# Keys by head parity and 64x64 products for the inverse, in a one-core language-model tower

## The reference

```
xr, xw, xk, xv, xa, xg = x + (x shifted by one token - x) * x_r, x_w, ...
r, k, v = xr @ Wr, xk @ Wk, xv @ Wv
w = -softplus(-(w0 + tanh(xw @ w1) @ w2)) - 0.5;  a = sigmoid(a0 + xa @ a1 @ a2);  g = sigmoid(xg @ g1) @ g2
kk = k * k_k, divided by its norm over each head;  k = k * (1 + (a - 1) * k_a)
for each token:  S = S * exp(-exp(w)) + (S @ -kk) (kk * a)^T + v k^T;   y = S @ r
out = (groupnorm(y) + sum(r * k * r_k) * v) * g @ Wo
```

## Time and profile before

| | |
|---|---|
| median of 3 runs | 646.49 us (645.17 to 652.29) |
| profiled execution | 646.06 us, its span 644.3 us |
| TensorE products, weight loads | 12883, 12884 |
| TensorE, VectorE, ScalarE, GpSimd busy | 491.5, 314.6, 236.7, 131.0 us |
| attention | 25.6 to 455.8 us |
| granted TensorE clock, mean | 0.858 |

### The profile page before, as it was taken

The page is one execution under the profiler, slowest core; times in us unless marked ns, Lnnn a source line. Parts: engine busy times, 40 slices in busy tenths (PEclk is TensorE's granted clock), DMA queues, the critical chain, the costliest instruction groups (busy, mean ns, idle before and its releaser), DMA issues.

```text
span 644.3 us, 28157 instructions
## 1 busy us (share of the span) xinstructions
PE 491.5 (76%) x12883; PEld 369.2 (57%) x12884; DVE 314.6 (49%) x686; ACT 236.7 (37%) x411; POOL 131.0 (20%) x117
## 2 busy tenths in 40 slices
PE   0196888798798798798798877786565899999910
PEld 0175676576686686576676666664432456676600
DVE  2356694674674585585565374242625312222213
ACT  2265644544444554453343440033320033333300
POOL 6421070240240140150040040100005400000054
PEclk9998989989888988979979877777785579999965
DMA  7700000000000000000000000000592211121135
GB/s 206 268 2 2 5 3 5 4 5 4 4 5 5 4 4 4 5 3 4 4 5 5 4 4 4 4 4 2 219 419 81 89 40 61 65 65 65 41 103 174
DMA packets 20680, 32.17 MB, mean 50 GB/s; under 512 B 3936, under 2 KB 16218, under 8 KB 20442
## 3 DMA queue, kind: packets, MB, share of 16 engines
q1 hardware_dynamic: 18234, 24.16, 10.6%
q0 software_dynamic: 2336, 6.30, 3.2%
HBM read 20.23 MB, written 10.22 MB: 47 GB/s over the span
## 4 chain that ended last, share of the span: by engine, by line
PE 70%; issue 13%; DVE 6%; ACT 5%; POOL 2%; DMA 1%; SPq 1%; POOLq 0%; DVEq 0%; ACTq 0%
PE ps L1152 7%; PE ps L1169 6%; PE ps L804 5%; PE ps L811 5%; PE ps L816 3%; PE ps L1132 2%; PE ps L825 2%; POOL arena L320 2%; PE ps L879 2%; PE ps L1160 2%; PE ps L872 1%; PE ps L868 1%; PE ps L1068 1%; PE ps L916 1%; PE ps L862 1%
## 5 line engine op out<-in xcount | busy, mean ns | idle before, releaser
L301 POOL TENSOR_TENSOR arena<-arena 128x512 f32<-128x512 f32 x8 | 11.0, 1380 | 244.3 <-ACT arena L394 244.3
L492 DVE SCALAR_TENSOR_TENSOR arena<-arena 128x256 f32<-128x256 f32 x96 | 49.7, 569 | 11.8 <-PE ps L855 8.0
L804 PE MATMUL ps<-arena 128*64 128x128 f32 x512 | 41.0, 327 | 7.7 <-ACT arena L386 4.1
L1152 PE MATMUL ps<-arena 128*128 x92 | 46.3, 628 | 0.1
L804 PEld LDWEIGHTS ps<-arena 128*64 128x64 f32 x512 | 37.3, 169 | 13.3 <-issue 8.9
L1169 PE MATMUL ps<-arena 128*128 x184 | 43.6, 380 | 0.8 <-ACT arena L453 0.8
L759 DVE TENSOR_TENSOR arena<-ps,arena 128x512 f32<-128x512 f32 x23 | 15.9, 692 | 48.0 <-PE ps L1152 48.0
L811 PE MATMUL ps<-arena 128*128 128x256 f32 x128 | 35.4, 423 | 5.1 <-ACT arena L423 5.0
L320 POOL DMA_INDIRECT arena<-sorted_o,arena x16 | 15.7, 980 | 113.4 <-DMA sorted_o<-arena 108.8
L1169 PEld LDWEIGHTS ps<-arena 128*128 128x128 f32 x184 | 33.2, 190 | 5.0 <-issue 1.5
L811 PEld LDWEIGHTS ps<-arena 128*128 128x128 f32 x128 | 25.2, 207 | 10.6 <-ACT arena L423 6.0
(11 more groups left out here) (249 smaller groups left out, 1161.1 us busy)
## 6 DMA issues: line engine op xcount, KB each, us to landing
arena<-W SPq DMA_DIRECT2D x16, 512.0 KB, 10.4
sorted_x<-arena SPq DMA_DIRECT2D x1, 2944.0 KB, 15.6
arena<-sorted_x SPq DMA_DIRECT2D x23, 128.0 KB, 2.0
sorted_o<-arena SPq DMA_DIRECT2D x23, 128.0 KB, 1.7
arena<-b SPq DMA_DIRECT2D x1, 2048.0 KB, 20.2
out<-arena SPq DMA_DIRECT2D x16, 128.0 KB
arena<-W SPq DMA_DIRECT2D x4, 256.0 KB
arena<-consts SPq DMA_DIRECT2D x4, 64.0 KB
```

What stands on the lines that cost most here:

```text
L492: last = V.scalar_tensor_tensor(out=mix[j % 3][:, p, :], in0=xx[:, p].rearrange("p b t -> p (b t)"), scalar=mixed_by[MIXES[j]][:, p:p + 1] ...
L804: last = mul(to, w[:, kt, half(h)], of_parity(src[:, kt, :], e), start=kt == 0, stop=kt == 1)
L1152: last = mm(ps[:, 2 + b, :], x_sT[b][:, p, :], W1_sb[:, bass.ds(e * (2 * HID) + p * HID, HID)], start=p == 0, stop=p == 1)
```

## The change

The change does the following.

- **Layout.** Keys, receptance, decay and the rest now stand as [2 heads x 64 features, chunk, batch, token]: partition half e is the head's parity. `headed` takes 128x128 stationary operands with all 256 columns, the a2 product too; P.cum takes four products with a block-diagonal `tri`; P.rt four products with two columns of `r_k_of`; `to_tokens` is four 128x128 transposes.
- **Inverse.** The products of Q.X and Q.T take two batches at a time: the stationary operand is 64x64, block-diagonal over two batches. For that GpSimd makes `n_w`, N spread over twice the columns (P.masks), and `y_t` is made twice as wide by the masks of VectorE, whose constants `low` and `parity` are widened.
- **P.M, Q.W, Q.S.** Products that read one head's rows run together, one half (or two batches) after the other, and TensorE waits on its own semaphores `m_half`, `w_half`, `s_half` between them.
- **Moved between engines.** ScalarE takes F.xn's two operations, k * k_k, the factor 1 + (a - 1) * k_a, and the floor under the norm (as Relu); GpSimd takes the centring of v (P.vc) and two operations of O.yn; VectorE gives these up.
- **Order.** `ORDER` is new, its numbers go from 3 to -1, and the waits follow it.

```diff
-ORDER = """Q.X0:0 P.vga:1 F.stats:3 Q.T0:0 P.lg:1 Q.A0:-1 P.wup:1 P.vc:0 Q.X1:0 Q.S0:-1 F.xx:2 Q.W1:-1 P.norm:1 Q.T1:0 P.key:1
-P.cum:1 Q.A1:-1 P.rt:0 F.rstd:3 Q.X2:0 Q.S1:-1 O.sq:-1 P.decay:1 P.g:1 O.red:-1 P.k:2 Q.T2:0 P.kP:1 P.ar:1 O.zT:-2
-P.bP:1 P.r:2 Q.X3:0 P.v:2 P.tokk:1 O.yn:-1 O.out:-2 P.M:1 F.xn:3 P.masks:1 P.tokb:1 P.q:1 P.lv:2 Q.T3:0 P.lwa:2
-O.add:-2 Q.W0:0 F.xT:3 P.kk:2""".split()
+ORDER = """P.q:0 Q.X0:0 F.rstd:2 P.r:1 F.xn:2 Q.T0:0 Q.A1:-1 P.norm:1 Q.X1:0 Q.S1:-1 O.sq:-1 O.red:-1 P.v:1 Q.T1:0 P.tokb:0
+P.lv:1 Q.X2:0 O.yn:-1 P.lwa:1 F.xT:2 Q.T2:0 P.vga:1 P.wup:1 Q.W0:0 F.xx:2 P.lg:1 P.key:1 Q.X3:0 O.zT:-1 P.cum:1 Q.T3:0
+P.decay:1 P.rt:1 P.ar:1 P.kP:1 P.bP:1 F.stats:3 Q.A0:0 P.g:1 Q.S0:0 P.k:2 P.M:1 P.masks:1 O.out:-1 Q.W1:0 P.vc:1
+O.add:-1 P.tokk:1""".split()
...
             def headed(w, src, bank):
 
-                for h in range(H):
+                for h2 in range(2):
                     for kt in range(2):
-                        for e in range(2):
-                            to = ps[half(e), bank, :].rearrange("p (h b c t) -> p h b c t", b=2, h=H, c=CH)[:, h]
-                            last = mul(to, w[:, kt, half(h)], of_parity(src[:, kt, :], e), start=kt == 0, stop=kt == 1)
+                        last = mul(pair(ps[:, bank, :], h2), w[:, kt, h2 * 128:(h2 + 1) * 128], src[:, kt, :], start=kt == 0, stop=kt == 1)
...
             def to_tokens(src, bank):
 
                 for c in range(CH):
-                    for h in range(H):
-                        for b in range(B):
-                            g, e, u = h * 2 + b // 2, half(b % 2), c * H + h
-                            last = mul(ps[quarter(b), bank, u * HS:(u + 1) * HS], src[e, g, c, :], ident[e, e], start=True, stop=True)
+                    for h2 in range(2):
+                        last = nc.tensor.transpose(ps[:, bank, c * C + h2 * 128:c * C + (h2 + 1) * 128], chunk(src, h2, c), ident)
...
                 elif step == "P.cum":
...
-                    for c in range(CH):
-                        for h in range(H):
-                            for b in range(B):
-                                q = quarter(b)
-                                to = ps[half(b % 2), 2 + b // 2, h * SL + c * L:(h + 1) * SL]
-                                last = mul(to, sig_w[q, c, half(h)], cst["tri"][q, 0:SL - c * L], start=c == 0 and h == 0, stop=c == 1)
+
+                    for h2 in range(2):
+                        mul(pair(ps[:, 2, :], h2), sig_w[:, 0, h2 * 128:(h2 + 1) * 128], cst["tri"], start=True, stop=False)
+                        last = mul(pair(ps[:, 2, :], h2)[:, 128:256], sig_w[:, 1, h2 * 128:(h2 + 1) * 128], cst["tri"][:, 0:128], start=False, stop=True)
...
                 elif step == "P.M":
...
+                    for hp in range(2):
+                        for part, (src, bank) in enumerate(((bP, 2), (kP, 3))):
+                            if hp:
+                                pe.wait_ge(s["m_half"], 2 * i + part + 1)
+                            for c in range(CH):
+                                for h in (hp, hp + 2):
+                                    for b in range(B):
+                                        u = c * H + h
+                                        last = mul(ps[quarter(b), bank, u * 2 * L:(u + 1) * 2 * L], chunk(src, h // 2, c)[half(hp), quarter(b)],
+                                                   ar[par][half(hp), h // 2, c, b, :], start=True, stop=True)
...
                 elif step == "Q.X0":
                     pe.wait_ge(s["u_ok"], 4 * i + 1)
-                    after(pe, "w_ok", 2 * i - 1)
+                    pe.wait_ge(s["nw_ok"], n)
+                    after(pe, "w_ok", 2 * i)
                     for u in range(UN):
-                        for b in range(B):
-                            q = quarter(b)
-                            last = mul(ps[q, 4, u * L:(u + 1) * L], n_b[par][q, u, 0:L], u_m[q, u, :], start=True, stop=True)
+                        for e in range(2):
+                            last = mul(ps[half(e), 4, u * L:(u + 1) * L], n_w[par][half(e), u].rearrange("p e t -> p (e t)"), u_m[half(e), u, :], start=True, stop=True)
...
+                    for h in (0, 2):
+                        for b in range(B):
+                            last = mul(ps[quarter(b), 4, half(h)], ar[par][half(0), h // 2, 0, b, 0:L], state[half(0), b, h // 2, :], start=False, stop=True)
+                    last.then_inc(s["w_half"], 1)
...
+                    pe.wait_ge(s["w_half"], 4 * i + 1)
+                    for h in (1, 3):
...
+                elif step == "P.masks":
+                    pool.wait_ge(s["nb_ok"], n)
+
+                    P.tensor_tensor(n_w[par], n_b[par][:, :, 0:L].unsqueeze(2).broadcast_to([128, UN, 2, L]), cst["parity"].rearrange("p (e t) -> p e t", e=2).unsqueeze(1).broadcast_to([128, UN, 2, L]), ALU.mult).then_inc(s["nw_ok"], 1)
+                elif step == "O.yn":
+                    pool.wait_ge(s["yn_ok"], n)
+                    P.tensor_tensor(yn, yn, gw[par], ALU.mult).then_inc(s["yg_ok"], 1)
+                    pool.wait_ge(s["yg_ok"], n)
+                    P.tensor_tensor(z, yn, qg[par], ALU.add).then_inc(s["z_ok"], 1)
...
+                elif step == "F.xn":
+                    act.wait_ge(s["res_ok"], n)
+                    act.wait_ge(s["lessm_ok"], n)
+                    for c in range(CH):
+                        last = A.activation(xn[:, c, :], xn[:, c, :], ACT.Identity, scale=rstd[:, c:c + 1], bias=less_mean[:, c:c + 1])
```

More of the change, by code:

```diff
@@ L131, in build @@
         tu = [carve(2, UN, L) for _ in range(2)]
-        y_t = carve(UN, L)
+        y_t = carve(UN, 2, L)
+        n_w = [carve(UN, 2, L) for _ in range(2)]
         w_s, sa = carve(C), carve(C)
@@ L935, in emit @@
                     for u in range(UN):
[L936 to L938 removed]
+                        for e in range(2):
+                            last = mul(ps[half(e), 6, u * L:(u + 1) * L], y_t[half(e), u].rearrange("p e t -> p (e t)"), t_m[half(e), u, :], start=True, stop=True)
                     last.then_inc(s["t_ps"], 1)
@@ L993, in emit @@
-                    for h in range(H):
-                        for b in range(B):
-                            g, e = h * 2 + b // 2, half(b % 2)
-                            last = mul(ps[quarter(b), 4, half(h)], ar[par][e, g, 0, 0:L], state[e, b // 2, half(h)], start=False, stop=True)
+                    for part, bank, at in ((0, 4, 0), (L, 5, 0 * C)):
+                        for h in range(H):
+                            for b in range(B):
+                                q, u = quarter(b), 0 * H + h
+                                mul(ps[q, bank, at + h * HS:at + (h + 1) * HS], m_k[par][q, u, part:part + L], vc[par][q, 0, half(h)],
+                                    start=h == 0 and (part == 0 or 0 == 0), stop=False)
@@ L997, in emit @@
+                    last.then_inc(s["w_half"], 1)
+                    pe.wait_ge(s["w_half"], 4 * i + 1)
+                    for h in (1, 3):
+                        for b in range(B):
+                            last = mul(ps[quarter(b), 4, half(h)], ar[par][half(1), h // 2, 0, b, 0:L], state[half(1), b, h // 2, :], start=False, stop=True)
                     last.then_inc(s["w_ps"], 1)
-                    for h in range(H):
+                    pe.wait_ge(s["w_half"], 4 * i + 2)
+                    for h in (1, 3):
@@ L1039, in emit @@
-                    pe.wait_ge(s["s_ok0"], n)
-                    for h in range(H):
-                        for b in range(B):
-                            g, e = h * 2 + b // 2, half(b % 2)
-                            last = mul(ps[quarter(b), 4, half(h)], ar[par][e, g, 1, 0:L], state[e, b // 2, half(h)], start=False, stop=True)
+                    for part, bank, at in ((0, 4, 0), (L, 5, 1 * C)):
+                        for h in range(H):
+                            for b in range(B):
+                                q, u = quarter(b), 1 * H + h
+                                mul(ps[q, bank, at + h * HS:at + (h + 1) * HS], m_k[par][q, u, part:part + L], vc[par][q, 1, half(h)],
+                                    start=h == 0 and (part == 0 or 1 == 0), stop=False)
@@ L1044, in emit @@
+                    last.then_inc(s["w_half"], 1)
+                    pe.wait_ge(s["w_half"], 4 * i + 3)
+                    for h in (1, 3):
+                        for b in range(B):
+                            last = mul(ps[quarter(b), 4, half(h)], ar[par][half(1), h // 2, 1, b, 0:L], state[half(1), b, h // 2, :], start=False, stop=True)
                     last.then_inc(s["w_ps"], 1)
-                    for h in range(H):
+                    pe.wait_ge(s["w_half"], 4 * i + 4)
+                    for h in (1, 3):
@@ L1213 @@
     col = np.arange(L)
+    pos = np.arange(B * SL)
+    heads, none = a[P + "r_k"], np.zeros((HS, 1), np.float32)
     f = np.float32
```

374 lines of the change are left out of this document (188 added, 186 removed).

## The result

The changed kernel takes **595.17 us** (median of 4 runs, 588.21 to 597.56) where the kernel before, on the same chip, takes 645.83: a ratio of 0.913, 95% interval 0.9004 to 0.9255. The ratio is taken over the faster executions of each kernel (590.7 and 647.0 us in the mean) and so is lower than 595.17 / 645.83 = 0.922. Forecast were 621 us; the sign was right and the gain was twice the forecast one.

What follows compares the result with a forecast made beforehand. TensorE's work and instruction delivery together were taken as the bound. A turn of 44.4 + 0.5 + 1.0 = 45.9 us against 49.96 brought attention from 430.2 to 405.5, hence 621 us; own range 606 to 636, 8 in 10 592 to 656.

Steps and rivals of the forecast that it cites:

- the end of the pauses: TensorE's idle time on instruction delivery in a steady turn: 0.5 us left of 6.7.
- the other waits: TensorE's waits for other engines, such as P.norm's table load and GpSimd's steps before O.zT: 1.0 us a turn added.
- the cover I was least sure of: GpSimd's widened N (1.5 us) before Q.X0: hidden by TensorE's work, but the one exposed first if that cover went.
- the clock term: TensorE in the steady turn: without pauses part of the lost clock returns, 2.0 us a turn, giving 44.4.
- TensorE's own sum: TensorE's busy time in a steady turn: the changed products and waits add 3.2 us to 43.25, giving 46.4.
- My upper end, 5.5: Most the clock could give back in a steady turn: all 5.5 us lost at a granted clock of 0.89.
- waits on its own half: TensorE waiting on its own earlier half, eight times in a slab: 0 to 2.0 us, taken as 0.6.
- the forecast's own half of 17.2 us idle: Attention's tail, 57.7 us with 17.2 idle: half the idle goes, leaving 48.5 us.
- Wide products are as good as their best rows: Rival, faster: inverse steps at 0.69 us, no own waits, half the others; 41.9 us a turn, about 595; chance 0.20.
- One row half at a time: Rival, slower: loads of one row group queue in P.M, Q.W, Q.S and inverse; 54.3 us a turn, about 676; chance 0.14.
- The pauses are not delivery: Rival, slower or same: 6.2 us more of TensorE's pauses stay; 52.1 us a turn, about 661; chance 0.04.
- Another engine takes over: Rival, same: GpSimd before Q.X0 and ScalarE's eight table loads cost 3.1 us a turn more, about 641; chance 0.12.

Runs made afterwards that it cites:

- after_again: The changed kernel itself, run again unchanged as the control of the second group: 591.49 us, ratio 0.9188.
- experiment 1: P.M's products done three times over in place: in the kernel before 703.03 us, in the changed kernel 665.89 us.
- before_m3: The kernel before with P.M's products done three times over in place: 703.03 us, ratio 1.0976.
- Experiments 1, 2 and 5: 2: the kernel before with 168 records fewer per slab, 609.42 us; 5: the changed kernel with four pauses a slab, 726.34 us, or one, 620.69 us.
- after_m3: The changed kernel with P.M's products done three times over in place: 665.89 us, ratio 1.0419.
- after_inv32_m3: The changed kernel with the inverse's products back at 32x32 and P.M's products done three times: 660.5 us, ratio 1.0219.
- after_inv32_tokb: The changed kernel with the inverse's products back at 32x32 and the copy of b's tokens moved from ScalarE to VectorE: 574.24 us, ratio 0.8908.
- after_pause: The changed kernel with four pauses of TensorE put into each slab, in four of the inverse's steps: 726.34 us.

## Why the forecast was right in its mechanism and wrong in its size

**What was right.** The bound (TensorE's work and delivery together), the counts (8499 products, 65 blocks), the end of the pauses (0.5 us a turn taken, 0.05 measured), the other waits (1.0 taken, 1.1 measured), VectorE 27.4, ScalarE 27.9, GpSimd 15.7 a turn for 27, 28, 16. GpSimd's widened N, the cover I was least sure of, was never late; three of TensorE's steps stand between P.M and Q.X0, not two.

**The step that failed is the clock term, "2.0", and with it TensorE's own sum, "46.4".** Together they gave 44.4 us busy a turn; measured were 39.9. Lines of the kernel before, of the same stretch as the earlier trace rows, show what the two consist of:

```profile
205.50 2.08 PE L879 MATMUL ps<-arena 128*128 128x256 f32 x4
...
210.33 0.75 PE L946 MATMUL ps<-arena 32*32 32x32 f32 x64
...
211.64 0.66 PE L1028 MATMUL ps<-arena 32*32 32x64 f32 x32
...
226.24 1.08 PE L1073 MATMUL ps<-arena 32*32 32x64 f32 x32
...
239.95 1.10 PE L916 MATMUL ps<-arena 64*32 64x64 f32 x64
240.87 1.07 PE L923 MATMUL ps<-arena 64*32 64x64 f32 x64
```

*Clock: 2.0 taken back, about 5.3 came.* L1028 and L1073 are the same shape at the full and at the lower clock, 0.66 and 1.08 us; L879's four wide records took 2.08 and take 1.14 in the kernel after. I added up each step's shortest time at the full clock, from its start to the next one's, over the four turns (L1068 and L1073, which have none, by L1023 and L1028): an estimate of 38.0 us of work a turn, where 43.25 were busy. Of the 5.3 between, 4.5 are in steps that ran at the lower clock in whole or part (11.1 us a turn were, 9.8 of them busy), and 0.8 in others, mostly steps that a pause broke in two. All of it went with the pauses: the clock is 1.00 and the changed kernel's busy 39.9 us are work. My upper end, 5.5, was right. I had the observation, a slow L816 behind paused small products, and did not draw what follows: if the pauses cause the low clock and the pauses go, the low clock goes too. The 2.0 was a hedge between two ends, not a mechanism. That is 3.3 of the 4.5 us.

*TensorE's own sum: +3.2 taken, +1.9 measured*, 38.0 to 39.9. By the same estimate, in us a turn:

| | taken | measured |
|---|---|---|
| keys and receptance | 0 | 0 |
| turns to tokens | -0.9 | -0.7 |
| a2 product | -0.3 | -1.4 |
| cumulative decay | +0.3 | 0 |
| r_k | 0 | +0.2 |
| inverse | +2.4 | +3.1 |
| P.M | +0.4 | -0.1 |
| Q.W | +0.4 | +0.1 |
| Q.S, with Q.A | +0.3 | +0.7 |
| waits on its own half | +0.6 | within the three above |

The a2 product was priced alone; it runs beside the values' product on other rows, and both together went from 2.4 to 1.07 us. The inverse's new step is 1.05 us from start to start, as taken; but the old one's 0.75 is the length to its last end, and the next step starts after 0.68 (L946 to L1023 at 211.01), so the term was too small. The same mistake is in P.M, where 2 x 1.10 counts an overlap twice: L916's start to L923's end is 1.99 us. The steps that now go one half of the rows after the other, with TensorE's waits on itself, cost 0.7 us together, for 1.7 taken, nearly all of it in Q.S. So the inverse's and Q.S's errors, which would have made the time longer, hid part of the others'.

In the stages: turns 1 to 5 took 41.4 + 164.0 = 205.4 us for 229.5 (-24.1), and the front 40.4 for 45 (-4.6; it got no longer by the later receptance, but shorter, which stays open). The other way went the tail, 52.4 for 48.5 (the forecast's own half of 17.2 us idle would have left 49.1), with a clock of 0.58 and one wait of 7.3 us on GpSimd, and turns 0 and 6, 1.8 together. Nothing is to be read from these two: in the profile of after_again they took 37.3 and 39.3 us for 41.5 and 42.8 here, with 3.1 and 0 us at the lower clock for 12.1 and 10.2, while the steady turns were the same. That is -23 in all, 382.5 for 405.5; with the kernel before's 430.2, the attention became 47.7 us shorter, and the two profiled executions differ by 48.5.

**The rivals.** *Wide products are as good as their best rows* had 595, and the time is 595.17, but that is luck: it had the inverse's step at 0.69, and it is 1.05. The time came by the clock, by the a2 product and by the halves that cost little. *One row half at a time* is refuted for P.M, 1.89 us for 1.99 before. The Trainium skill's page "TensorE: Matmul & The Clock Gate", "Part 3: Packing small matmuls", says that loads overlap products in flight only when the row group differs. P.M, with up to four products on one row half, shows no such price. *The pauses are not delivery* is refuted by experiment 1, with 3.7 us from block to block. The Trainium skill's page "Runtime: NRT & Kernel Launch", "Instruction fetch mechanics", has the cost of crossing into a new block mostly hidden. The changed kernel agrees (65 blocks, 0.2 us of "issue" in four turns); before_m3 and the kernel before do not. *Another engine takes over*: true of two short waits only, 0.75 us a turn for ScalarE and 0.3 for VectorE.

**What the change does, by the runs.** In a steady turn, idle time falls from 6.7 to 1.1 us and the lower clock with the broken steps (5.3 us by the estimate above) goes, while the work grows by 1.9: 9.0 us a turn. Experiments 1, 2 and 5 show the two links, from dense small products to pauses and from pauses to the clock. That the 256 records of the inverse were needed for it is refuted: with them narrow the kernel is some 7 us faster once ScalarE's late copy is out of the way. How the rest divides between the 292 other records, the new order and the work moved between engines was not measured.

## What to carry to other kernels

Count TensorE's instructions against a block's time as an engine of its own: an fp32 product is two records with two loads. A block was delivered in 3.7 us, so a row of small products that runs through 256 instructions in 2 us will stand once it is longer than what lies ready; here 128 records in a row did not, and of 384 the first 229 ran. The sum over a turn is not enough to count: with 9.75 blocks a turn the waits on "issue" were 0.8 us in one kernel and 2.6 in another, by how densely the products stood. Price a pause by what stands behind it as well: four pauses of about 2 us a turn cost 2.4 times themselves, one of 2 us between 0.7 and 11.7 us. When a change takes the pauses away, take the whole clock back in the sum. Widen small products until the dense rows have room, and not further: for the inverse, four narrow tiles side by side were faster than two wide ones. And take a step's time from its start to the next one's start, not to its own last end.

## What the runs showed of the hardware, not expected

- 256 instructions a block, 3.73 us from one to the next under a waiting TensorE, in after_m3, before_m3 and after_inv32_m3 alike. Behind eight wide products 229 records with their loads, 1.8 blocks, ran before the first stop, in 3.31 us; part of them can have arrived meanwhile.
- The clock stayed at 1.00 for 1250 records a turn, most of them small (after_inv32_tokb), and fell to 0.75 with four pauses of about 2 us a turn (after_pause, 209 to 270 us).
- 128 products in one row half and then the other took 1.89 us, against 1.99 with the halves in turn; a 33-row and a 64-row product ran as pairs, four pairs in 1.06 us.
- 64 products of 32x32 (0.76 us) were a third faster than 32 of 64x64 (1.12).
